# Layer 1 matmuls behind more units of TensorE's order, in a fused embedding, bilinear and MLP kernel

## The reference

```python
e = jnp.stack([tbl_f[ids[:, f]] for f in range(40)], axis=1)          # 512 x 40 x 32
z = jnp.einsum('bpd,pde,bpe->bp', e[:, iidx, :], matrices, e[:, jidx, :])  # 512 x 780
h = jnp.concatenate([z, dense_ctx], axis=1)                           # 512 x 796
h = jnp.maximum(h @ W_top1 + b_top1, 0.0)                             # 796 x 512
h = jnp.maximum(h @ W_top2 + b_top2, 0.0)                             # 512 x 256
y = h @ W_top3                                                        # 256 x 1
```

## Time and profile before

| | us |
|---|---|
| median of 3 runs | 198.24 (198.16 to 199.68) |
| the profiled execution | 198.23 |
| its span, first to last instruction | 196.3 |

### The profile page before, as it was taken

How to read it: one execution, slowest core, us unless ns; L and a number is a source line. 1 busy time by engine, 2 the same in 40 slices (tenths; PEclk the granted TensorE clock), 3 DMA queues, 4 the chain that set the end, 5 groups by cost and what they waited for, 6 DMA issues and landing times.

```text
span 196.3 us, 3798 instructions
## 1 busy us (share of the span) xinstructions
PE 182.7 (93%) x1624; PEld 55.1 (28%) x1624; DVE 149.8 (76%) x148; ACT 56.3 (29%) x58; POOL 106.1 (54%) x114
## 2 busy tenths in 40 slices
PE   3996969599899999999999999999999999998992
PEld 1232313133222322222223222322322322222340
DVE  4869989966798996685699997776969996664502
ACT  4997389993110101112101011201111011112401
POOL 6877777877777777777777777822001002213000
PEclk9999999999999999999999999999999999999999
DMA  5930030300669240051000001000000000000000
GB/s 150 404 133 17 13 94 13 110 12 17 199 179 342 54 147 17 13 159 16 12 13 17 13 13 17 14 0 0 5 0 0 3 0 0 5 0 0 3 0 0
DMA packets 6921, 10.83 MB, mean 55 GB/s; under 512 B 2004, under 2 KB 4440, under 8 KB 6904
## 3 DMA queue, kind: packets, MB, share of 16 engines
q1 hardware_dynamic: 3832, 9.00, 13.7%
q0 software_dynamic: 3072, 1.58, 4.5%
HBM read 10.57 MB, written 0.00 MB: 54 GB/s over the span
## 4 chain that ended last, share of the span: by engine, by line
PE 72%; DVE 1%; ACT 0%; issue 0%; DVEq 0%
PE ps_t L634 27%; PE ps_z L648 24%; PE ps_x L672 10%; PE ps_t L628 4%; PE ps_t L683 4%; PE ps_t L657 2%; PE ps_x L608 2%; DVE prod L556 0%; PE ps_z L692 0%; ACT late_z L477 0%; DVE prod L559 0%; DVEq L555 0%
## 5 line engine op out<-in xcount | busy, mean ns | idle before, releaser
L546 DVE TENSOR_TENSOR prod<-ps_t,xt 128x1024 f32<-128x1024 f32 x100 | 115.6, 1216 | 27.7 <-PE ps_t L634 22.3
L434 POOL DMA_INDIRECT emb<-tbl,idx x96 | 93.8, 978 | 29.6 <-issue 28.9
L634 PE MATMUL ps_t<-xt,w_sb 32*128 32x512 f32 x360 | 58.8, 640 | 0.0
L648 PE MATMUL ps_z<-prod,ones 128*32 128x512 f32 x400 | 53.0, 604 | 0.0
L442 POOL TENSOR_TENSOR late_z<-late_z,tbl_oh 128x512 f32<-128x512 f32 x8 | 10.2, 1277 | 44.6 <-ACT tbl_oh L484 44.6
L634 PEld LDWEIGHTS ps_t<-xt,w_sb 32*128 32x128 f32 x360 | 19.8, 182 | 34.2 <-issue 20.3
L672 PE MATMUL ps_x<-late_z,late_w 128*32 128x512 f32 x192 | 22.8, 592 | 0.0
L503 DVE TENSOR_SCALAR hot_dve<-ids,ramp 128x2048 bf16<-128x2048 f16 x27 | 18.9, 754 | 1.5 <-PE ps_x L596 1.5
L648 PEld LDWEIGHTS ps_z<-prod,ones 128*32 128x32 f32 x400 | 8.1, 108 | 37.9 <-issue 30.3
L484 ACT ACTIVATE tbl_oh<-ps_x 128x512 f32<-128x512 f32 x8 | 4.8, 597 | 40.4 <-PE ps_x L672 40.4
L477 ACT ACTIVATE late_z<-ps_z 128x512 f32<-128x512 f32 x7 | 4.2, 594 | 35.3 <-PE ps_z L648 35.3
(11 more groups left out here) (65 smaller groups left out, 84.5 us busy)
## 6 DMA issues: line engine op xcount, KB each, us to landing
tbl_oh<-small_tables SPq DMA_DIRECT2D x3, 512.0 KB, 4.5
emb<-tbl,idx POOLq DMA_INDIRECT x96, 2.3
late_w<-w SPq DMA_DIRECT2D x1, 1280.0 KB
late_w<-w SPq DMA_DIRECT2D x2, 512.0 KB, 5.0
w_sb<-w_pairs SPq DMA_DIRECT2D x1, 704.0 KB, 4.2
tbl_oh<-small_tables SPq DMA_DIRECT2D x1, 640.0 KB, 6.8
w_sb<-w_pairs SPq DMA_DIRECT2D x1, 640.0 KB, 3.9
w_sb<-w_pairs SPq DMA_DIRECT2D x1, 576.0 KB, 4.1
```

The costliest lines, as they stand in the source:

```text
L434: nc.gpsimd.indirect_dma_start(emb[:, n % E_RING, t, u * D:(u + 1) * D], None, tables[field], bass.IndirectOffsetOnAxis(ap=idx[:, at:at + ...
L546: nc.vector.tensor_tensor(prod[:, g % PROD_RING, :].rearrange("p (i b) -> p i b", i=2), ps_t[PAIR[g]][:, :].rearrange("p (i b) -> p i b", ...
L634: last = nc.tensor.matmul(o, w_sb[s * D:(s + 1) * D, at:at + P], xt[s * D:(s + 1) * D, kk, :], start=True, stop=True)
L648: last = nc.tensor.matmul(ps_z[q * D:(q + 1) * D, :], ones[:, v * D:(v + 1) * D], prod[:, t // 2 % PROD_RING, t % 2 * B:(t % 2 + 1) * B], ...
```

## The change

The list `EARLY` gets a number of its own for each of the eight steps of a pair of chunks, and `early_at` no longer repeats a number for both steps of a sum. All else follows from the plan.

```diff
-EARLY = [((0, 1), (26, 30, 34, 40)), ((2, 3), (56, 62, 68, 76)), ((4, 5), (88, 92, 96, 99))]
+
+EARLY = [((0, 1), (27, 31, 35, 38, 40, 44, 48, 51)), ((2, 3), (57, 59, 63, 66, 70, 72, 74, 76)),
+         ((4, 5), (83, 89, 91, 93, 95, 97, 99, 99))]
 LATE = [(6, 0), (6, 1), (6, 2), (6, 3)]
```

```diff
-    early_at = [at for chunks, ats in EARLY for at in ats for _ in chunks]
+    early_at = [at for chunks, ats in EARLY for at in ats]
+    assert all(len(ats) == M1 * len(chunks) for chunks, ats in EARLY)
```

## The result

| | before | after |
|---|---|---|
| median of 6 runs each, us | 198.31 (198.16 to 200.32) | 196.78 (195.46 to 197.32) |
| ratio on record, after to before | | 0.9848, 95% interval 0.9805 to 0.9891 |
| the profiled execution, us | 198.23 | 196.99 |
| its span, mean granted clock | 196.3, 1.000 | 195.2, 0.991 |

What follows compares the result with a forecast made beforehand. It took TensorE and VectorE waiting for each other, VectorE slower per bare unit, as the bound. From 198.23 us it subtracted 3.03 us of covered stall, with visit starts, layer 1 work and open bank at nothing: 195.2 us, range 194.4 to 196.7.

Steps and rivals of the forecast that it cites:

- The stall that a visit covers: TensorE's pairs in groups 28 to 99: each visit wipes the following pair's wait, 5.82 us falling to 2.79, 3.03 less.
- a second pair behind a single visit: Second pair of groups after a one-matmul visit: wait taken as 0.38 us, with 0.20 and 0.49 as the sides.
- What a visit costs to begin: Start of the 11 added layer 1 visits on TensorE: taken as 0; from above 1.3 or 3.3 us.
- change of shape: Rival: each added visit pays 0.12 us for switching matmul shape, 1.3 us in all, giving 196.5 us; chance 0.08.
- exposed start: Rival: loader gaps of 0.3 to 0.8 us uncovered at each added visit, up to 204.0 us; chance 0.04.
- The 0.12 of the prediction: TensorE's change from 128-row to 32-row shape: about 0.12 us, already paid once per unit and only moved behind the visit.
- The stall comes back elsewhere: Rival: the lead limit sets the total and VectorE's pace returns each wait later; no gain, 198.2 us; chance 0.07.
- What bounds the kernel now: TensorE and VectorE waiting for each other in turn; VectorE slower per bare unit, 2.26 us against 2.07; stall 5.82 us.
- the lead limit: Limit of three pair tiles that TensorE meets at the second pair after VectorE runs dry: 1.45 us against 1.07.
- the 0.20 of the later pairs: Each pair after the second follows VectorE's pace, taking 1.27 us in place of 1.07.
- The median is 198.24, so no correction: Base time of the whole kernel: profiled execution 198.23 us matches the median of the runs, so 0 us is added.
- What would show it: Signs in the changed profile: listed pair and visit lengths, less VectorE idling, loader waits below 20.8 us, first part's length unchanged.

Runs made afterwards that it cites:

- the repeat: The changed kernel run once more with no edit; ratio to the kernel before 0.9854 (0.9810 to 0.9899).
- `placed`: Changed kernel with its layer 1 steps, still mostly single, moved in front of units that wait; median 195.91 us, ratio to the kernel before 0.9773.
- `doubles`: Kernel before with its 12 visits of two layer 1 steps kept whole but moved to other groups; median 198.37 us, ratio 0.9934.
- `m448_before`: Kernel before with the last 64 of 512 samples left out of each VectorE multiply from group 6 on; 110.26 us from transpose 5 to the last copy.
- `m448_after`: Changed kernel with the last 64 of 512 samples left out of each VectorE multiply from group 6 on; 108.44 us from transpose 5 to the last copy.

## Why the prediction was right, and where it was not

**The stall that a visit covers: right to the row.** 5.82 us of waits, 2.79 left, 3.03 gained; measured 2.98 in the profiled stretch, and again in the repeat, with each of the 34 pairs as listed. The value for which there had been no row, a second pair behind a single visit, was 0.38, as taken. `placed`, `doubles` and the visits of 0.22 us show the rule by itself: the smaller of wait and visit is saved, once for each place.

**What a visit costs to begin: nothing, as taken.** 0.86 a step in the chain, and equal stretches without waits. So the rivals "change of shape" and "exposed start" are out. The 0.12 of the prediction was read from two rows of the chain that don't prove it, since the chain shows about 1.00 for a burst in front of a visit too (79.28); the starts bear it out, 1.00 against 0.88. The Trainium skill ("TensorEngine Tiling (Array Packing)", Key Properties) has a drain at each change of mode; that is in line with this case, where burst and visit share a mode and the number of changes stayed. No run here put a visit between two other modes.

**The stall comes back elsewhere: out.** It didn't, nor did any transfer, bank or ring begin to wait.

**What bounds the kernel now: right in its numbers, incomplete in its reason.** I began with VectorE being slower in a bare unit, 2.26 against 2.07, and called the 0.38 the lead limit. `m448_before` parts them: with VectorE faster than TensorE the second pairs still wait, 0.24, since the round trip of a pair tile is longer than a unit. Pace sets only the 0.20 of the later pairs, and even of that a part stays when VectorE is faster. For this change the sum is the same either way; for a change to the multiply it is not.

**"The median is 198.24, so no correction": the step that failed.** The absolute time went by one profiled execution and three runs, two of them of the shortest kind. Later runs of the same kernel had a median of 199.7, 24 of 35 with a mean clock under 1.000. The forecast of 195.2 is what the changed kernel takes at clock 1.000 (195.29 and 195.46); its medians are 1.3 and 1.6 us above. The range had no term for this: its upper end, 196.7, stands there for other reasons, and the first median, 196.78, lies just beyond it. That the time came so near to it is in part luck, by the kinds that the six runs caught. The two medians of the first table, 1.53 us apart, show how far six runs a side can mislead, when they catch the kinds of execution unevenly.

**What would show it:** all came, but for two. The part before the first visit didn't keep its length, 75.88 against 74.05, by the clock. The loader's waits for VectorE were to fall from 20.8 and rose to 44.9, since that view puts a name to a gap that is there in any case.

## What to carry to other kernels

Where two engines pass tiles to each other through a short ring, read the waits as pieces of the chain by position, and put independent work in front of each place that waits: it is free up to the length of that wait, and a second piece in the same place covers nothing. Work out the round trip of a tile (start to reader, reader, handover back) beside the paces of the engines; the ring waits if either is longer than the time between reuses. And ask how much the kernel before scatters from run to run before trusting an absolute figure. The two ratios on record, 0.9848 and 0.9854, agree to 0.001, closer than their intervals of 0.004 to either side would ask for, while the median of before went from 198.3 to 199.7.

## What the runs showed of the hardware

- The granted clock of TensorE isn't repeated from run to run. In three of the 14 profiles it fell to half (1.2 GHz) for 3.4 us, beginning between 38.0 and 38.7 us, in the sparse one-hot part. In `after` that costs 1.2 us. The mean clock that goes with it, about 0.991, stood in 18 of 35 executions of the kernel before, which took 1.5 to 2.6 us more than its shortest, a late rise included.
- Full speed sets in between 12.7 and 16.0 us from the start in the profiles of this study; the latest cost 1.3 us. The mean granted clock doesn't tell it: it reads 1.000 in two profiles with a rise at 15.8 and 16.0 us (`doubles`, `m448_after`). Three profiles with a mean of 0.997 had the rise at 13.9 to 16.0 us and a fall in their last 0.9 to 1.2 us, when TensorE had no work left, which costs nothing.
- From the start of a pair on TensorE through VectorE's multiply of 128 x 1024 fp32 elements back to TensorE it takes 1.18 + 1.23 + 0.05 = 2.46 us, the round trip that the second pairs wait for.
- Eleven more switches between a half-filled accumulation bank and others, at the same shape of the matmul, change the stretch by 0.01 us in all (101.06 and 101.05).
